# Eight linear-attention layers of a perceiver: another issue order on TensorE, ScalarE and VectorE

## The reference, cut to what matters

```python
for i in range(8):
    residual = x
    Q = elu(x @ Wq[i] + bq[i]) + 1            # feature map
    Kf = elu(x @ Wk[i] + bk[i]) + 1
    V = x @ Wv[i] + bv[i]
    KV, sumK = (Kf * V).sum(seq), Kf.sum(seq) # elementwise, no matrix per head
    att = Q * KV / (Q * sumK + 1e-6)
    x = layer_norm(gelu(att @ Wo[i] + bo[i]) + residual)
    residual = x
    h = gelu(gelu(x @ W1[i] + b1[i]) @ W2[i] + b2[i])
    x = layer_norm(h + residual)
```

## Time and profile before

| | us |
|---|---|
| median of three runs | 2918.47 |
| lowest and highest | 2912.57, 2923.48 |
| the profiled execution's own time | 2930.86 |
| its span, first to last instruction | 2929.1 |
| TensorE busy over the span | 2466.0 (84%) |
| VectorE busy | 2273.9 (78%) |
| ScalarE busy | 1855.2 (63%) |
| GpSimd busy | 851.9 (29%) |
| mean granted TensorE clock | 0.895 |

### The profile page before, as it was taken

How to read it: one execution, slowest core, us unless ns; L and a number is a source line. 1 busy time by engine, 2 the same in 40 slices (tenths; PEclk the granted TensorE clock), 3 DMA queues, 4 the chain that set the end, 5 groups by cost and what they waited for, 6 DMA issues and landing times. The chain is left out here.

```text
span 2929.1 us, 34847 instructions
## 1 busy us (share of the span) xinstructions
PE 2466.0 (84%) x11811; PEld 1388.3 (47%) x11811; DVE 2273.9 (78%) x3098; ACT 1855.2 (63%) x2579; POOL 851.9 (29%) x478
## 2 busy tenths in 40 slices
PE   6789999998799999999999999997345676555997
PEld 3356666664244444444444444443124565344675
DVE  3587777773799999999999999994669998465554
ACT  4355555554698898888889998885334554213443
POOL 1021212110444443444444444441001000301554
PEclk8989999999899999999999999998566776656999
DMA  1010000000100000000000000000000110200211
GB/s 56 1 33 15 19 15 15 19 4 11 69 0 0 37 0 37 0 36 0 37 0 36 0 27 10 0 1 11 0 20 22 36 34 10 90 22 28 75 60 43
DMA packets 25494, 68.10 MB, mean 23 GB/s; under 512 B 3128, under 2 KB 15224, under 8 KB 23928
## 3 DMA queue, kind: packets, MB, share of 16 engines
q1 hardware_dynamic: 25344, 66.23, 6.6%
HBM read 60.91 MB, written 5.31 MB: 23 GB/s over the span
## 5 line engine op out<-in xcount | busy, mean ns | idle before, releaser
L251 PE MATMUL a_ps<-a_x,a_w 128*128 128x512 f32 x1536 | 696.2, 598 | 25.2 <-DVE a_kf L599 12.9
L251 PEld LDWEIGHTS a_ps<-a_x,a_w 128*128 128x128 f32 x1536 | 291.7, 191 | 405.1 <-issue 367.9
L774 POOL TENSOR_TENSOR a_den<-a_qf,a_ksum 128x1024 f32<-128x1024 f32 x128 | 271.1, 2118 | 512.0 <-DVE a_qf L592 475.4
L777 POOL TENSOR_TENSOR a_num<-a_qf,a_kvsum 128x1024 f32<-128x1024 f32 x128 | 294.9, 2304 | 185.4 <-DVE a_kvsum L617 185.4
L2307 DVE TENSOR_REDUCE x_rn<-x_sqk 128x8 f32<-128x512 f32 x256 | 174.3, 681 | 106.6 <-ACT x_sqk L2231 102.4
L2231 ACT ACTIVATE x_sqk<-x_b_k 128x512 f32<-128x512 f32 x256 | 153.1, 598 | 157.2 <-PE x_b_k L2143 150.8
L262 PE MATMUL a_ps<-a_att,a_w 128*128 128x512 f32 x480 | 215.8, 592 | 0.0
L592 DVE SCALAR_TENSOR_TENSOR a_qf<-a_eq,a_qf 128x1024 f32<-128x1024 f32 x128 | 195.4, 1526 | 1.7
L2124 POOL TENSOR_TENSOR x_kn<-x_craw,x_w 128x256 f32<-128x256 f32 x64 | 47.0, 734 | 511.0 <-DVE x_craw L2296 489.3
L445 ACT ACTIVATE a_den<-a_den,consts 128x1024 f32<-128x1024 f32 x128 | 147.0, 1149 | 55.8 <-POOL a_den L774 55.8
L599 DVE SCALAR_TENSOR_TENSOR a_kf<-a_ek,a_ps 128x1024 f32<-128x1024 f32 x128 | 155.5, 1215 | 29.8 <-ACT a_ps L441 22.7
(11 more groups left out here) (399 smaller groups left out, 5380.8 us busy)
## 6 DMA issues: line engine op xcount, KB each, us to landing
a_w<-layers SPq DMA_DIRECT2D x8, 2577.0 KB, 9.4
x_craw<-ctx SPq DMA_DIRECT2D x32, 256.0 KB, 2.7
y_cx<-ctx_t SPq DMA_DIRECT2D x16, 512.0 KB, 3.5
m_wb<-m_scratch SPq DMA_DIRECT2D x16, 512.0 KB, 3.9
m_w<-experts SPq DMA_DIRECT2D x8, 544.0 KB, 4.9
x_w<-xattn_w SPq DMA_DIRECT2D x1, 2048.0 KB, 7.5
x_all<-x_t SPq DMA_DIRECT2D x1, 1024.0 KB, 5.0
t_scratch<-t_q_t SPq DMA_DIRECT2D x4, 256.0 KB, 3.7
```

The source lines that it names most:

```text
L251: last = nc.tensor.matmul(bank(tile, j), col(par, part * HK + u * P, P), x[:, t0:t0 + BANK], start=True, stop=True)
L774: nc.gpsimd.tensor_tensor(by_batch(den[:, b, :]), by_batch(qf[:, b, :]), bcast(ksum[:, b, :], S), ALU.mult).then_inc(d_ready, 1)
L777: nc.gpsimd.tensor_tensor(by_batch(num[:, b, :]), by_batch(qf[:, b, :]), bcast(kvsum[:, b, :], S), ALU.mult).then_inc(n_ready, 1)
```

## The change

In the three lists the entries are put into another order. No operation, wait, tile or line of a helper is changed, and GpSimd's and SyncE's programs are the same. On TensorE k(0) goes ahead of q(0), v(0), v(1) and v(3) go earlier by one entry, k(3) goes ahead of the first mean, v(5) from behind `down(1)` to between `up(1)` and `up(2)`, `down(0)` behind q(5), and k(7) ahead of v(6). On ScalarE k(0) goes ahead of q(0), k(3) ahead of the first square, `inverse(2)` ahead of q(4), `inverse(5)` ahead of q(7). On VectorE most units have their entries in another order.

```diff
--- before.py
+++ after.py
@@ -329,44 +329,44 @@
         if not half:
             pe.wait_ge(w_loaded[par], 4 * v - 8 * par + 16)
         wait_ahead(pe, affine, 2 * v - 2)
+        k_of(0)
         q_of(0)
-        k_of(0)
+        v_of(0)
         out(2)
-        v_of(0)
         q_of(1)
         k_of(1)
+        v_of(1)
         out(4)
-        v_of(1)
         k_of(2)
         out(6)
         q_of(2)
         v_of(2)
+        k_of(3)
         norm(mean, 0)
-        k_of(3)
+        v_of(3)
         q_of(3)
         norm(var, 0)
-        v_of(3)
         k_of(4)
         q_of(4)
         v_of(4)
         up(0)
         up(1)
+        v_of(5)
         up(2)
         up(3)
         if tail:
             pe.wait_ge(hid_gelu, 4 * tv + 2)
         k_of(5)
-        down(0)
         if tail:
             pe.wait_ge(hid_gelu, 4 * tv + 3)
         q_of(5)
+        down(0)
         down(1)
         k_of(6)
-        v_of(5)
         q_of(6)
         norm(mean, 1)
+        k_of(7)
         v_of(6)
-        k_of(7)
         norm(var, 1)
         q_of(7)
         v_of(7)
@@ -506,13 +506,13 @@
         of_tail(gelu_out, tv, tp)
         q_of(2)
         inverse(1)
+        k_of(3)
         of_tail(square, 2 * tv)
-        k_of(3)
         q_of(3)
         of_tail(rsqrt, 2 * tv)
         k_of(4)
+        inverse(2)
         q_of(4)
-        inverse(2)
         of_tail(gelu_hidden, tv, tp)
         k_of(5)
         inverse(3)
@@ -524,8 +524,8 @@
         of_tail(square, 2 * tv + 1)
         k_of(7)
         of_tail(rsqrt, 2 * tv + 1)
+        inverse(5)
         q_of(7)
-        inverse(5)
         inverse(6)

     def tail_alone(v, par):
@@ -673,70 +673,70 @@
         sums_k(0)
         clips_q(0)
         features_q(0)
+        features_k(1)
         if tail:
             attend(8 * v - 1, 1, th, CH - 1, tv)
-        features_k(1)
+        clips_q(1)
         sums_kv(0)
-        clips_q(1)
         features_q(1)
+        products_kv(1)
         sums_k(1)
-        products_kv(1)
         features_k(2)
+        sums_kv(1)
+        if tail:
+            add_residual(2 * tv, x_of(th), 2 * tv)
+        products_kv(2)
         sums_k(2)
         if tail:
-            add_residual(2 * tv, x_of(th), 2 * tv)
-        attends(0)
-        sums_kv(1)
-        if tail:
             centre(2 * tv)
-        products_kv(2)
         clips_q(2)
         features_q(2)
         features_k(3)
+        attends(0)
+        products_kv(3)
         sums_kv(2)
-        products_kv(3)
         if tail:
             normalise(2 * tv, x1[:, :], bias(tp, C_S1), bias(tp, C_B1))
         features_k(4)
+        products_kv(4)
+        clips_q(3)
+        attends(1)
         sums_k(3)
-        attends(1)
-        clips_q(3)
         attends(2)
+        features_q(3)
+        clips_q(4)
+        sums_k(4)
         sums_kv(3)
-        clips_q(4)
-        features_q(3)
-        sums_k(4)
         features_q(4)
-        products_kv(4)
+        sums_kv(4)
         features_k(5)
+        products_kv(5)
         sums_k(5)
         attends(3)
         clips_q(5)
-        sums_kv(4)
-        features_q(5)
+        sums_kv(5)
         if tail:
             add_residual(2 * tv + 1, x1[:, :], 2 * tv + 1)
-        products_kv(5)
-        sums_kv(5)
+        features_q(5)
         features_k(6)
         if tail:
             centre(2 * tv + 1)
         sums_k(6)
+        attends(4)
+        clips_q(6)
+        features_q(6)
         products_kv(6)
-        clips_q(6)
-        attends(4)
-        features_q(6)
         features_k(7)
-        sums_kv(6)
+        sums_k(7)
         if tail:
             normalise(2 * tv + 1, x_of(th), bias(tp, C_S2), bias(tp, C_B2))
-        sums_k(7)
+        sums_kv(6)
         products_kv(7)
+        sums_kv(7)
+        clips_q(7)
+        features_q(7)
         attends(5)
-        clips_q(7)
-        sums_kv(7)
         attends(6)
-        features_q(7)

     def tail_alone(v, par):
         parts = [slice(j * BANK, (j + 1) * BANK) for j in range(2)]
```

## The result

The kernel after takes 2943.03 us in the median of six runs (2939.89 to 2951.2), the kernel before beside it 2920.97 (six runs, 2912.57 to 2930.64): a ratio of 1.0077, with a 95% interval of 1.0052 to 1.0102. It is slower, by 15 to 30 us, that is by 0.5 to 1%. The forecast was 2935 us, in a range of 2906 to 2952.

What follows compares the result with a forecast made beforehand. TensorE's order of work and its waits set the pace; +1.57 us a window (23.6 over fifteen), +0.7, -5.2 and -2.5 once sum to +16.6 us, taking the median from 2918.47 to 2935, range 2906 to 2952.

Steps and rivals of the forecast that it cites:

- (a): Window's end and first projection: TensorE's wait for the last normalisation (L642) goes, -0.73 us a window.
- (b): v(5) between the ups: the fourth up no longer waits for the first gelu, -0.45 us a window.
- (c): k(3) ahead of mean(0): the mean no longer waits for the residual sum, -0.38 us a window.
- (d): One block fewer between var(0) and up(0): L642 clashes with GpSimd's multiply, up(0) waits, +1.41 us a window.
- (e): v(5) gone from behind down: ScalarE's gapless chain from down(1) to var(1) leaves a hole, +1.72 us a window.
- The rule on the shared port: First normalisation: VectorE and GpSimd exclude each other, issue order decides who blocks; stall taken whole, half would give 2924.
- The end of the back edges: Two windows after the loop's back edge: VectorE's slack before F 1 (features_k) swallows the jump, -5.2 us once.
- The end of the stage: Closing sequence: GpSimd's last denominator starts at 9.0 us instead of 11.5, -2.5 us once.
- window 0: First window, bound by VectorE: comes out within half a microsecond, 0 (bounds -2.6 and +3 us).
- No clash: Rival at the first normalisation: V 2 (sums_kv) and L639 fall apart, 21 us less, 2914, no change; chance 0.20.
- never waits: Rival: TensorE's waits go or are hidden, window falls to 75.5 us, total 2873; chance 0.15.
- worse: Rival: thin cover missed or residual sum meets GpSimd, back edges stay; about 1 us a window more, 2950; chance 0.20.

Runs made afterwards that it cites:

- b_v6_behind: Kernel before, with sums_k(7) ahead of the last normalisation and sums_kv(6) behind it on VectorE: ratio to before 0.9972, window 77.39 us.
- h_after_before: Lists of the kernel after up to v_of(4), gelu_hidden and features_k(4), those of the kernel before from there: ratio to before 1.0015, window 78.65 us.
- a_early_v2: Kernel after, with attends(0) ahead of the first centre and sums_kv(2) ahead of products_kv(3) on VectorE: ratio to before 1.0011, window 78.27 us.
- a_flat: Kernel after, with windows 1 to 12 written out instead of the hardware loop: ratio to before 1.0064, windows 80.09 us.
- a_all: a_both with the gelu table set ahead of the wait at all three gelus: ratio to before 0.9882, window 75.65 us.
- a_k7_back: Kernel after, with v_of(6) ahead of k_of(7) on TensorE again: ratio to before 1.0082, window 79.62 us.
- a_preload: Kernel after, with ScalarE loading the third gelu's table ahead of its wait for down(1): ratio to before 1.0011, window 78.33 us.
- a_both: a_early_v2 plus second square ahead of q(6), v(6) ahead of k(7), products_kv(6) ahead of clips_q(6): ratio to before 0.9959, window 76.93 us.

## Why the prediction was right, step by step

**The window.** 79.7 us were forecast from 78.12 + 1.57; it takes 79.62. *(a)* The wait on L642 is gone; L642 ends 1.65 us into the window (1.5 forecast), long ahead of k(0). b_v6_behind prices it alone at 0.74 (0.73 forecast). *(b)* The fourth `up` waits no more; h_after_before shows that (d) would have removed this wait as well. *(c)* The wait of the first mean for the residual sum is gone. *(d)* From mean(0) to up(0) 13.26 us (1314.80 to 1328.06), 13.3 forecast, where seven blocks are 12.0; a_early_v2 prices it at 1.35 (1.41 forecast). *(e)* From the end of `down(1)` to var(1) 11.21 us (1347.05 to 1358.26), 11.22 forecast, and the hole in the places named: beyond the pitch 0.63 us at mean(1) (0.5 forecast), 1.68 at k(7) (1.5) and 0.41 at var(1) (0.4).

**The rule on the shared port** spoke for taking the clash at its whole price and not at half. In all 15 windows the wait comes, though in the loop GpSimd begins only 0.01 us behind L639 (0.10 forecast). In the three windows behind the loop GpSimd is first: there L642 lasts 0.81, which the prediction had named as a sign of being wrong, and L639 2.50, and the wait is 0.53. The case that the prediction gave for the other order of issue, that L639 and not L642 would wait and that the end would hardly change, appears in a_flat, where L639 comes after GpSimd has begun (first VectorE, then GpSimd):

```profile
1401.16 2.50 DVE L639 SCALAR_TENSOR_TENSOR a_z<-a_z,a_g 128x1024 f32<-128x1024 f32 x1 [0.57 <-ACT a_g L466]
1403.70 0.81 DVE L642 TENSOR_SCALAR a_x<-a_z,a_w 128x1024 f32<-128x1024 f32 x1
```

```profile
1400.67 1.91 POOL L777 TENSOR_TENSOR a_num<-a_qf,a_kvsum 128x1024 f32<-128x1024 f32 x1 [0.41 <-DVE a_kvsum L617]
```

GpSimd keeps its 1.91, L639 takes 2.50 in place of 1.23 and ends 1.08 us behind GpSimd's end, L642 keeps its 0.81. It ends 13.67 us behind the mean's start, where it ended 13.20 in the kernel after, with the root ready 0.66 later: the price is nearly the same, as forecast. By the rule of the Trainium skill (SBUF — State Buffer, Who interferes with whom) the order of issue decides who is blocked; the two traces agree, one for each order.

**The end of the back edges: this step failed.** The 14 windows had extras of 6.4 us and were to keep 1.2; 1120.27 - 14 x 79.62 = 5.6 are left. The term of -5.2 measured -0.8. The prediction looked at VectorE's 2.61 us at the jump and found slack for them. But ScalarE has a jump of its own, longer, and in the new order k(0) stands ahead of q(0) in its list: q(0) comes behind the pause and behind 2.0 us of k(0). ScalarE behind the jump:

```profile
1453.03 1.11 ACT L440 ACTIVATE a_ek<-a_ps,a_w 128x1024 f32<-128x1024 f32 x1 [4.67 <-issue]
1454.05 1.08 ACT L441 ACTIVATE a_ps<-a_ps,a_w 128x1024 f32<-128x1024 f32 x1
1455.04 1.12 ACT L433 ACTIVATE a_eq<-a_ps,a_w 128x1024 f32<-128x1024 f32 x1
```

and TensorE, which wants to write q(1) into the tile of q(0):

```profile
1457.22 5.42 PE L251 MATMUL a_ps<-a_x,a_w 128*128 128x512 f32 x12 [1.90 <-ACT a_qf L434]
```

The window behind a jump costs 2.05 and 2.17 us more than its neighbours, as before (2.03, 2.05), at another tile. In the kernel before it was 0.90 at k(1), which the earlier trace rows have, and 1.15 more at the first mean, which the prediction overlooked. That the jumps cause this is shown by a_flat, where it is gone; that it is ScalarE's jump is read from the two rows above, and no run took one engine's jump away alone.

**The end of the stage: mis-sized.** Forecast -2.5 from an attend that comes earlier; the last denominator starts 8.4 us into the stretch (9.0 forecast, 11.5 in the kernel before), and the wait for its attend (L376) fell from 4.72 to 2.53, that is 2.2, near the forecast. But the stretch fell from 55.90 to 50.77, 5.1 us. The rest is TensorE's clock: the kernel before was granted 0.86 of the full 2.4 GHz in that stretch, so for part of it the lower level of 1.2 GHz, the kernel after 0.93. The stretch of the kernel before, in the columns of the earlier trace rows:

```profile
1983.80:2039.70 55.90, 42.30 (x81) 16.08 (x80) 25.25 (x30) 28.03 (x36) 6.95 (x4) 0.86 0.00 0
```

The 16 passes at L392 take 8.80 us before and 7.10 after, the four at L376 3.78 and 2.47; first the kernel before, then after:

```profile
2000.80 3.78 PE L376 MATMUL a_ps<-a_att,a_w 128*128 128x512 f32 x4 [4.72 <-DVE a_att L624]
...
2013.77 8.80 PE L392 MATMUL a_ps<-a_x,a_w 128*128 128x512 f32 x16 [1.70 <-DVE a_x L642]
```

```profile
2018.74 2.47 PE L376 MATMUL a_ps<-a_att,a_w 128*128 128x512 f32 x4 [2.53 <-DVE a_att L624]
...
2030.57 7.10 PE L392 MATMUL a_ps<-a_x,a_w 128*128 128x512 f32 x16 [1.51 <-DVE a_x L642]
```

Of the 14 profiled kernels only before and a_all show 8.80; h_after_before, with before's end and its wait of 4.73 at L376, has 7.11. So 1.7 of the 5.1 belongs to the profiled execution and not to the order. The four passes at L376 vary too: 2.47 to 3.48 us in the six kernels that end as after does, behind the same wait of 2.53; how much of the 1.3 us there is the order's stays open.

**The sum.** The forecast for the stage was +16.6. Without window 0 the two traces show +17.2 (from 806.29 to 2039.70, and from 804.15 to 2054.80): the failed term (+4.4) was offset by the mis-sized one (-2.6), and by 14 windows of +1.50 in place of +1.57 (-1.0). The first window with a tail took its +2.2 (77.41 to 79.61) as forecast. Window 0, put at 0 within half a microsecond, took 65.91 us in place of 64.13, which makes +19.0 for the stage. In a_k7_back, whose edit only exchanges two late blocks of TensorE, it takes 67.69 at a granted clock of 0.88 in place of 0.91, so how much of the 1.8 us is the order's stays open. That the total came out well is luck to the extent of the failed and the mis-sized term. Outside the stage, where the program is the same, the profiled execution of the kernel after took 9.8 us less, which is why the two spans differ by 9.2 only. The medians differ by 22.1, in an interval of 15 to 30; what of the 3 us above 19.0 is real, no row says.

**The rivals.** "No clash" and "never waits" fell with the wait at L289 in every window and with the hole; of "worse", only the back edges came true. The measured 2943 lies 2 us above the forecast's own range (2929 to 2941) and inside the wide one (2906 to 2952); "slower" had the largest chance, 0.48.

## What to carry to other kernels

Cost a new order by following one period of the bounding engine through its pitches and hand-overs: single waits of 0.4 to 1.7 us were right within 0.2 this way, while shares of busy time pointed the wrong way. When a block of cover is moved, ask which chain on another engine it had covered, and shorten that chain (a table load ahead of its wait, the needed operation first) rather than move the wait about. At a loop's back edge look at every engine, and when the steady state has no slack left, try it without the loop.

## What the runs showed of the hardware that was not expected

- ScalarE stands still for 3.3 to 5.6 us at the loop's jump, VectorE for 2.61, and the pause isn't the same from kernel to kernel (3.3 to 3.5 before, 4.55 to 4.67 after, 5.6 in b_v6_behind), with nothing that the trace names. What reaches TensorE differs too: 2.0 us in the kernel before, 5.9 and 7.0 in a_all, which otherwise has no waits. Part of it is TensorE's clock. In a_early_v2 the two jumps stop TensorE for 1.84 and 1.92 us; behind the first twelve passes take 5.42 us at a granted clock of 1.00, behind the second 7.11 at 0.76, and the windows are 2.1 and 3.9 us longer. In a_k7_back a pause of 2.65 was followed by 5.42.
- An activation table load takes 1.28 us, and one that precedes a gelu may or may not run ahead of the wait for the gelu's input; in the loop the first gelu's load ran ahead (0.02 us of idle time in front of it), written out it waited (1.32). Setting the table by hand ahead of the wait put all of them ahead of it, in a_preload and in a_all.
- After a pause of TensorE of 2.5 to 2.7 us the next four passes took from 1.98 to 3.55 us (L376 in a_all and in a_both, pause 2.73 in both). These two kernels have the same list on TensorE. The clock after such a pause isn't fixed by that list; what decides it stays open.
